# Expert weights loaded per tile as the stationary operand, hidden activations made transposed, and shared-expert units regrouped

## The reference, cut to what matters

```python
x = x + tanh(g_xattn) * attention(layernorm(x), ctx)      # 8192 tokens x 128
flat = layernorm(x)
scores = softmax(flat @ router_w.T + router_bias)         # 32 experts
topk_scores, topk_idx = top_k(scores, 4)                  # normalised to sum 1
h = silu(flat @ gate_w[e].T) * (flat @ up_w[e].T)         # width 128, per expert e
expert_out = h @ down_w[e].T
out = sum over the token's four experts of topk_score * expert_out
out = out + silu(flat @ sgate_w.T) * (flat @ sup_w.T) @ sdown_w.T   # shared, width 512
x = x + tanh(g_ffn) * out
```

## Time and profile before

| | us |
|---|---|
| runs | 1081.31, 1076.92, 1077.49; median 1077.49 |
| the profiled execution | 1076.78, its span 1074.9 |
| attention | 0 to 565 |
| early stage | 565 to 592 |
| expert loop, to the last scatter | 592 to 997 |
| late stage | 997 to 1075 |

### The profile page before, as it was taken

The page is one execution under the profiler, slowest core; times in us unless marked ns, Lnnn a source line. Parts: engine busy times, 40 slices in busy tenths (PEclk is TensorE's granted clock), DMA queues, the critical chain, the costliest instruction groups (busy, mean ns, idle before and its releaser), DMA issues.

```text
span 1074.9 us, 26031 instructions
## 1 busy us (share of the span) xinstructions
PE 954.3 (89%) x6592; PEld 728.6 (68%) x6593; DVE 733.7 (68%) x2496; ACT 613.1 (57%) x2213; POOL 669.9 (62%) x935
## 2 busy tenths in 40 slices
PE   4988888988888888889769999999999999999987
PEld 2777777777777777777655666666667666776544
DVE  3788888888888988888755344444444444454696
ACT  3667766767677777767532455555555555555211
POOL 1267777777777777777662477677777677777100
PEclk9999999999999999999879899999999999999999
DMA  5511111111111111111315433333333333331794
GB/s 154 200 37 33 36 37 37 33 33 39 36 36 33 39 38 33 39 38 62 110 33 98 99 96 95 95 91 90 94 93 96 93 92 93 93 94 32 273 363 146
DMA packets 91623, 90.43 MB, mean 84 GB/s; under 512 B 21277, under 2 KB 73098, under 8 KB 91204
## 3 DMA queue, kind: packets, MB, share of 16 engines
q1 hardware_dynamic: 71876, 55.07, 18.4%
q0 software_dynamic: 17408, 33.87, 9.6%
q10 hardware_dynamic: 2304, 1.07, 0.6%
HBM read 49.72 MB, written 42.31 MB: 86 GB/s over the span
## 4 chain that ended last, share of the span: by engine, by line
PE 43%; DVE 17%; issue 16%; DMA 12%; POOL 9%; ACT 1%; POOLq 1%; SPq 0%; DVEq 0%; ACTq 0%
DMA x_rows<-payload,slot 11%; PE ps L1071 11%; POOL x_rows L432 9%; PE ps L1082 9%; DVE payload L751 3%; PE ps L1108 3%; PE ps L1066 3%; PE ps L1076 3%; PE ps L1092 3%; PE ps L1098 3%; PE ps L1035 2%; DVE kvbd L677 2%; PE ps L942 2%; DVE w_gu L881 1%; PE ps L1044 1%
## 5 line engine op out<-in xcount | busy, mean ns | idle before, releaser
L443 POOL DMA_INDIRECT y_rows<-y_sb,xin x288 | 283.0, 983 | 141.8 <-issue 80.5
L432 POOL DMA_INDIRECT x_rows<-payload,slot x256 | 251.2, 981 | 132.7 <-DVE slot L762 70.4
L836 DVE TENSOR_TENSOR h<-sg,ps 128x128 f32<-128x128 f32 x288 | 82.6, 287 | 181.6 <-ACT sg L575 181.6
L1071 PE MATMUL ps<-w_gu,xT 128*128 x576 | 175.9, 388 | 8.2 <-issue 8.2
L1082 PEld LDWEIGHTS ps<-w_dn,hT 128*128 128x128 f32 x576 | 94.4, 190 | 105.8 <-ACT hT L580 73.0
L942 PE MATMUL ps<-vt,pT 128*128 128x108 f32 x1024 | 145.6, 287 | 0.0
L580 ACT COPY hT<-ps 128x128 f32<-128x128 f32 x288 | 76.4, 265 | 109.7 <-PE ps L1076 107.4
L942 PEld LDWEIGHTS ps<-vt,pT 128*128 128x128 f32 x1024 | 130.7, 200 | 11.3 <-issue 10.9
L1082 PE MATMUL ps<-w_dn,hT 128*128 x576 | 129.9, 308 | 8.1 <-DVE y_sb L842 6.2
L575 ACT ACTIVATE sg<-ps 128x128 f32<-128x128 f32 x288 | 80.5, 280 | 72.7 <-PE ps L1071 48.8
L842 DVE TENSOR_SCALAR y_sb<-ps,xin 128x128 f32<-128x128 f32 x288 | 99.7, 346 | 24.2 <-PE ps L1082 22.5
(11 more groups left out here) (136 smaller groups left out, 1978.4 us busy)
## 6 DMA issues: line engine op xcount, KB each, us to landing
xin<-x_rows SPq DMA_DIRECT2D x288, 65.0 KB, 1.9
w_gu<-y_rows SPq DMA_DIRECT2D x16, 1024.0 KB, 8.6
y_rows<-y_sb,xin POOLq DMA_INDIRECT x288, 2.3
w_gu<-in_gu SPq DMA_DIRECT2D x2, 2048.0 KB, 10.3
x_rows<-payload,slot POOLq DMA_INDIRECT x256, 2.4
out<-x_all SPq DMA_DIRECT2D x16, 256.0 KB, 5.8
w_dn<-in_dn SPq DMA_DIRECT2D x1, 2048.0 KB, 8.8
ctx_sb<-in_ctxT SPq DMA_DIRECT2D x64, 29.2 KB
```

The lines of the kernel that those rows point to most:

```text
L432: nc.gpsimd.indirect_dma_start(x_rows, bass.IndirectOffsetOnAxis(ap=slot[:, v, k:k + 1], axis=0), payload[:, v, k, :], None).then_inc(sent ...
L443: nc.gpsimd.indirect_dma_start(y_rows, bass.IndirectOffsetOnAxis(ap=xin[:, u, D:D + 1].bitcast(U32), axis=0), y_sb[:, u, :], None, bounds_ ...
L836: nc.vector.tensor_tensor(h[:, u % 2, :], sg[:, u % 2, :], ps_gu[u % 2][:, H:2 * H], ALU.mult).then_inc(h_d[u % PER], 1)
L1071: after(nc.tensor.matmul(ps_gu[u % 2][:, 0:2 * H], xT[:, u % 2, :], w_gu[:, bass.ds(e * (2 * H), 2 * H)], start=True, stop=True), xT_d, n, ...
```

## The change

**Weights per tile.** `w_gu` and its two loads are gone. `w_t` (in a new tensor `moe`, on which the result slots lie too) has 18 slots of 256 columns. For each tile SyncE issues a load of that expert's 128 KB, then the load of `xin`; both raise the same semaphore, so its counts go by 32. A row reads 18 first rows and 21 expert numbers. The first row is split: tiles 0 to 3 first, then 4 to 17.

**Transposed hidden.** `gate_up` is two products now, with the weights stationary and `xT` moving, so that the hidden activations come out transposed. `turn_h` on TensorE and the copy `h_turned` on ScalarE are gone. Three banks and buffers (`DEEP` = 3) take turns instead of two. `down` and `result` come for the tile three before the current gate/up, and ahead of it in the order.

**Shared units.** `EARLY` is 1, `MID` 11. Four units stand in a row, at tiles 1, 5, 9 and 13, one whole chunk per row, in rows 1 to 6 and 8 to 12. Rows 0, 7, 13, 14 and 15 have none. Four chunks are left for the late stage.

**Paddings and scatters.** ScalarE issues four paddings per early unit instead of two; SyncE issues 12 before the table is stored and 4 after (before 8 and 8). GpSimd waits for each tile's result instead of for every second.

```diff
-EARLY = 2
-MID = 8
+EARLY = 1
+MID = 11
-UNIT_AT = (6, 14)
+DEEP = 3
+UNIT_AT = (1, 5, 9, 13)
...
         def bodies(body, fori):
-            body(0, 0, 0, first=True)
-            body(1, 0, 1)
-            with fori(1, MID - 1) as c:
-                body(2 * c, c, 0)
-                body(2 * c + 1, c, 1)
-            body(TG - 2, MID - 1, 0)
-            body(TG - 1, MID - 1, 1, last=True)
+            body(0, first=True)
+            with fori(1, 7) as j:
+                body(j, chunk=EARLY - 1)
+            body(7)
+            with fori(8, 13) as j:
+                body(j, chunk=EARLY - 2)
+            with fori(13, TG - 1) as j:
+                body(j)
+            body(TG - 1, last=True)
...
-                     2: lambda: sp.dma_start(w_gu[:, 0:half], gu[:, 0:half]).then_inc(s_moe, 16),
-                     3: lambda: sp.dma_start(w_gu[:, half:], gu[:, half:]).then_inc(s_moe, 16),
...
-            def load_tiles(j):
-                firsts = numbers(sp, tab_sb, j * TW, U3, XROWS - 128)
-                for u in range(U3):
+            def load_tiles(j, begin=0, end=U3):
+                firsts = numbers(sp, tab_sb, j * TW + begin, end - begin, XROWS - 128)
+                es = numbers(sp, tab_sb, j * TW + EAT + begin, end - begin + 3, E - 1)
+                for u in range(begin, end):
                     need(sp, y_sent[u], 16 * j)
-                    sp.dma_start(xin[:, u, :], x_rows[bass.ds(firsts[u], 128), :]).then_inc(xin_in[u], 16)
-            load_tiles(0)
+                    sp.dma_start(w_t[:, u, :], gu[:, bass.ds(es[u - begin + 3] * (2 * H), 2 * H)]).then_inc(xin_in[u], 16)
+                    sp.dma_start(xin[:, u, :], x_rows[bass.ds(firsts[u - begin], 128), :]).then_inc(xin_in[u], 16)
+            load_tiles(0, 0, 4)
+            load_tiles(0, 4, U3)
...
             def scatter(n, u):
-                if u % 2 == 0:
-                    need_first(pool, y_d[(u + 1) % PER], n[(u + 1) // PER + 2])
+                need_first(pool, y_d[u % PER], n[u // PER + 2])
...
-            def gate_up(n, u, e):
-                after(nc.tensor.matmul(ps_gu[u % 2][:, 0:2 * H], xT[:, u % 2, :], w_gu[:, bass.ds(e * (2 * H), 2 * H)],
-                                       start=True, stop=True), xT_d, n, u).then_inc(gu_p[u % PER], 1)
+            def gate_up(n, u):
+                after(nc.tensor.matmul(ps_gu[u % DEEP][:, 0:H], w_t[:, u % U3, 0:H], xT[:, u % 2, :],
+                                       start=True, stop=True), xT_d, n, u)
+                nc.tensor.matmul(ps_gu[u % DEEP][:, H:2 * H], w_t[:, u % U3, H:2 * H], xT[:, u % 2, :],
+                                 start=True, stop=True).then_inc(gu_p[u % PER], 1)
...
             def body(j, first=False, last=False, chunk=None):
                 n = counts(dve, j, U3 // PER)
                 for u in range(U3):
+                    if not (first and u < 3):
+                        result(n, u - 3)
                     hidden(n, u)
-                    if not (first and u < 2):
-                        result(n, u - 2)
-                    if u - 2 in UNIT_AT:
-                        mixed_hidden(c, 2 * half + UNIT_AT.index(u - 2))
-                if half:
-                    mixed_take(c)
+                    if chunk is not None and u - 1 in UNIT_AT:
+                        mixed_hidden(j + chunk, UNIT_AT.index(u - 1))
+                if chunk is not None:
+                    mixed_take(j + chunk)
```

More of the change, by code:

```diff
@@ L332, in _ @@
             sp.dma_start(tab_dram, tab[0:TG, :]).then_inc(t_store, 16)
-            with sp.Fori(2, PADS_SP // 4) as e:
-                paddings(e)
+            paddings(PADS_SP // 4 - 1)
             sp.wait_ge(t_store, 16)
@@ L559, in _ @@
             for n in range(4 * EARLY):
-                if n % 2 == 0:
-                    firsts = numbers(act, basei, PADS_SP + 2 * n, 4, XROWS - 128)
-                for first in firsts[2 * (n % 2):2 * (n % 2) + 2]:
+                for first in numbers(act, basei, PADS_SP + 4 * n, 4, XROWS - 128):
                     act.dma_start(x_rows[bass.ds(first, 128), :], pad[:, :]).then_inc(t_padded2, 16)
@@ L574, in silu, with mixed_silu @@
                 tile_done(act, gu_p, n, u)
[L575 to L583, removed]
+                nc.scalar.activation(sg[:, u % DEEP, :], ps_gu[u % DEEP][:, 0:H], ACT.Silu).then_inc(sg_d[u % PER], 1)
+            def mixed_silu(c, k):
+                unit = 4 * c + k
                 need(act, sg_p, 2 * unit + 1)
@@ L586, in mixed_silu, with body @@
                 nc.scalar.activation(ssg[:, k % 2, :], ps_g[:, :], ACT.Silu).then_inc(ssg_d, 1)
-            def body(j, c, half, first=False, last=False):
+            def body(j, first=False, last=False, chunk=None):
                 n = counts(act, j, U3 // PER + 1)
@@ L591, in body @@
                     silu(n, u)
-                    if not (first and u == 0):
-                        h_turned(n, u - 1)
                     if not (last and u >= U3 - 2):
                         evac(n, u + 2)
-                    if u in UNIT_AT:
-                        mixed_silu(c, 2 * half + UNIT_AT.index(u))
+                    if chunk is not None and u in UNIT_AT:
+                        mixed_silu(j + chunk, UNIT_AT.index(u))
             for u in range(2):
@@ L857, in mixed_take, with body @@
                                                op0=ALU.mult, op1=ALU.add).then_inc(take_d, 4)
-            def body(j, c, half, first=False, last=False):
+            def body(j, first=False, last=False, chunk=None):
                 n = counts(dve, j, U3 // PER)
                 for u in range(U3):
+                    if not (first and u < 3):
+                        result(n, u - 3)
                     hidden(n, u)
-                    if not (first and u < 2):
-                        result(n, u - 2)
-                    if u - 2 in UNIT_AT:
-                        mixed_hidden(c, 2 * half + UNIT_AT.index(u - 2))
-                if half:
-                    mixed_take(c)
+                    if chunk is not None and u - 1 in UNIT_AT:
+                        mixed_hidden(j + chunk, UNIT_AT.index(u - 1))
+                if chunk is not None:
+                    mixed_take(j + chunk)
             bodies(body, dve.Fori)
-            for u in range(2):
-                result(counts(dve, TG), u - 2)
+            for u in range(3):
+                result(counts(dve, TG), u - 3)
             def combine(c):
@@ L1079, in down, with units @@
             def down(n, u, e):
                 tile_done(pe, y_d, n, u - 1)
-                after(nc.tensor.matmul(ps_dn[:, 0:D], hT[:, u % 2, :], w_dn[:, bass.ds(e * D, D)], start=True,
+                after(nc.tensor.matmul(ps_dn[:, 0:D], hT[:, u % DEEP, :], w_dn[:, bass.ds(e * D, D)], start=True,
                                        stop=True), hT_d, n, u).then_inc(dn_p[u % PER], 1)
-            def units(j, k):
-                unit = 4 * (EARLY + j) + k
+            def units(c, k):
+                unit = 4 * c + k
```

104 lines of the change are left out of this document (48 added, 56 removed).

## The result

The changed kernel takes 1096.1 us (median of four runs, 1090.72 to 1098.5); the kernel before took 1079.4 beside it. The ratio is 1.0143, with a 95% interval of 1.0088 to 1.0197: slower by 1.4%, where 1082 us, 0.4%, was forecast. The measured median lies outside the forecast's own 1073 to 1092 and inside the range for 8 in 10, 1056 to 1098, near its upper end.

What follows compares the result with a forecast made beforehand. Expert loop bound by TensorE in chunk rows, GpSimd in others: from 617.5, rows to 943.2, last scatter 1015.4, tail 63.5, end 1078.9; with 1.9 around it and the median's footing, 1082 us. Range 1073 to 1092; 8 in 10, 1056 to 1098.

Steps and rivals of the forecast that it cites:

- rival B: In the expert loop SyncE's loads become the bound, from 0.67 us per load: rows take 27.9, total 1098; chance 0.18.
- A unit's four tiles: In the expert loop, four tiles with a shared unit, delayed by VectorE's wait, take 6.2 to 6.3 us.
- the delayed down: In a unit's group, TensorE's down waits for a result behind VectorE's product: 4.44 us, where it was due at 4.03.
- Rival A: In the expert loop VectorE's wait does not delay the down: groups take 5.7 us, rows 25.6, total 1057; chance 0.27.
- Rival C: In the late stage TensorE waits some 8 us for the first combine, returning at 0.50 clock: total 1087; chance 0.05.
- The tail: From the last scatter to the end, with fewer late units and an earlier first combine: 63.5 us instead of 78.0.
- The start: Before the steady loop: first load near 588.5, about 1.8 us gained; row 1's first tile taken at 617.5.
- from 617.5: In the loop's sum, row 1's first tile starts then; eleven chunk rows and row 7 follow, ending at 943.2.
- Chunk rows: The eleven expert-loop rows with four shared units each: 27.6 to 28.1 us, taken as 27.9.
- plain row 7: The expert-loop row without shared units, between the chunk rows: TensorE takes 18.8 us.
- the ring: Plain tiles' chain from gate/up to the next but one: 1.96 us for two; a row above 20 disproves it.
- From row 13's first gate product to its first scatter: Near the loop's end, three tiles, down, result and issue put the first scatter about 4 us later.

## Why the prediction was right, and what it mis-sized

**The range was held in part by luck.** The forecast alone, with its own terms, ended at 1092; 1096.1 is beyond it. The range for 8 in 10 reached to 1098 because it went to half of rival B, and B did not happen. That the change is slower had 0.46; the forecast value of 0.4% was itself within the 0.5% that the prediction counted as no change.

**The mechanism held.** A unit's four tiles were put at 6.2 to 6.3 and measure 6.32; the tile with the gate 1.63 and 1.64; the delayed down at 4.44 from the group's start and 689.98 - 685.43 = 4.55. L841 starts 0.13 after the up product's end where 0.05 was counted; the difference is about the 0.1 that was priced for register instructions. Rival A needed groups under 5.9 and falls by the rows; the runs with the product later (-18 us) and with two banks (-26 us, against the 25 that A was priced at) show what it would have been; the second also shortens plain tiles, as shown below. Rival B needed SyncE as long as TensorE's row: a row of 36 loads takes 22.4 to 22.7 where SyncE isn't held up, as forecast with 22.3, and 0.52 per load, and with the same loads the rows fall to 23.2 in two of the runs. The Trainium skill's rule for large transfers (DMA: Bandwidth & Descriptors, section Measured (HBM→SBUF, 128 partitions, SWDGE, issued from GpSimd)) does not decide here: the run without the bytes is as slow. Rival C was half there: TensorE did wait for the first combine, but for 3.27 us instead of some 8 (1037.61 above); until 1034.3 it had its late units to do. In this window the clock stayed at its 2.4 GHz level, 1.00 (columns as above):

```profile
1034.00:1042.00 8.00, 4.43 (x22) 2.76 (x22) 7.55 (x10) 0.72 (x2) 0.00 (x0) 1.00 1.03 379
```

The tail was put at 63.5 and is 62.5.

**What was mis-sized is the loop, by 11 us of the profiled span** (1078.9 forecast, 1088.9 measured, with 1.0 back from the tail):

- The start, 3.3. The first load was put at 588.5 and came at 589.88, though the attention's last scatter was 0.9 earlier; in all ten kernels here it comes 17.6 to 19.0 after that scatter, where 588.5 meant 16.4. This cost the sum nothing, since it took the later of its two cases: the second row's loads were due at 611.7 + 3.2 = 614.9 and began at 614.30. What the step "from 617.5" left out comes behind them. In TensorE's order the transposes of the row's first two tiles stand ahead of its first gate product. The second waits for its load until 618.55, and from there to the gate product are 2.25 more: 620.80.
- Chunk rows, 4.6. They were put at 27.9 and take 28.3 on the mean. Four groups are 25.3, so 2.9 to 3.1 are left in most rows for two more tiles, the row's start and the take, where 2.85 were counted. With 6.3 per group the forecast's own terms add up to 28.05, and 27.9 was taken.
- The plain row 7, 1.7, which takes TensorE 20.5 instead of 18.8 (18 x 0.98 + 1.03 is 18.7). A plain row above 20 was to prove the ring wrong, and it came. The ring itself is short by 0.03 per tile, as the rows below show, which makes 0.6. The rest lies at the row's edges: the second reading of numbers, 0.92 in TensorE's queue, holds up one tile by 0.6 and was not counted, and the row's first tile and the change to the next row add 1.65 where 1.0 was counted.
- From row 13's first gate product to its first scatter, 1.3: 5.3 instead of 4.

Here are two plain tiles of row 7, from a gate product (L1061) to the next but one:

```profile
793.31 0.39 PE L1061 MATMUL ps<-xT,moe 128*128 128x128 f32 x2
...
794.00 0.48 PE L1069 MATMUL ps<-w_dn,hT 128*128 x2
...
794.52 0.35 DVE L833 TENSOR_SCALAR y_sb<-ps,xin 128x128 f32<-128x128 f32 x1
...
795.01 0.48 PE L1069 MATMUL ps<-w_dn,hT 128*128 x2
...
795.33 0.39 PE L1061 MATMUL ps<-xT,moe 128*128 128x128 f32 x2
```

The forecast's ring takes 2.02 for two tiles instead of 1.96: VectorE's result starts 1.21 after the gate product, not 1.15; the 0.49 and 0.32 behind it are as forecast. A second ring closes in the same 1.01 per tile, which the forecast did not name: a down (794.00), its result 0.52 later, the next down 0.49 after that. Which of the two sets the tile can't be told from these rows; both pass through the one bank. With two banks the plain tiles of the same row are (789.13 - 784.11)/6 = 0.84 apart, so the one bank prices plain tiles as well as units:

```profile
784.11 0.39 PE L1062 MATMUL ps<-xT,moe 128*128 128x128 f32 x2
...
789.13 0.39 PE L1062 MATMUL ps<-xT,moe 128*128 128x128 f32 x2
```

**The rest, some 5 us, lies outside the profiled execution.** The median of the four executions is 5.4 above the profiled one, and the forecast was made on the footing of a profile 0.7 below the median. In the ten profiled executions of all kernels here the attention's last scatter starts between 569.9 and 578.3, though the code of that stage is the same but for the two weight loads; from there to the end the change and the three runs that gave nothing all take 517 to 518 us, the kernel before 502.8. The three longer executions of the change have a lower granted clock over the whole span, 0.956 to 0.960 instead of 0.965. They were not profiled, so that they lost their time in the attention is likely, and not shown.

## What to carry to other kernels

An instruction that waits in an in-order queue charges everyone behind it: before a product is moved nearer to its producer, look at what stands next on that engine and who waits for that, and through which buffer. Background work was free here up to the pace of the slowest engine in each row (23.2 us) and dear beyond it, so it is better spread evenly to that pace than gathered in a few rows. A buffer that has one slot is worth a look even where no wait is large: here a second bank took 0.17 off a plain tile and 0.49 off the four tiles of a unit. A load that lands a row ahead may move many bytes for nothing.

## What the runs showed of the hardware that was not expected

In the attention most batches take 8.1 us, but between six and twelve take 8.8 to 11.0. There are two kinds.

The 29th and the 57th are long in all ten profiled executions, 10.0 to 10.1 and 10.2 to 11.0 us. In the change GpSimd stands 2.2 us instead of 0.30 before the second scatter of both, for a reason that the profile doesn't show. The clock is not the cause: it is at its 2.4 GHz level through the 29th batch of the change (first its late scatter, then the window of the batch, columns as above).

```profile
280.45 0.97 POOL L435 DMA_INDIRECT x_rows<-payload,slot  x1 [2.17 <-issue]
```

```profile
277.00:287.00 10.00, 7.34 (x67) 6.10 (x66) 7.67 (x31) 6.25 (x21) 6.06 (x10) 1.00 0.09 30
```

The others lie at other places in each execution. In the one from 345 to 354 of the change, of 9.2 us, all scatters are on time, but for 3 us TensorE runs at its 1.2 GHz level, busy throughout:

```profile
347.00:350.00 3.00, 3.00 (x16) 3.00 (x16) 2.47 (x9) 1.53 (x6) 2.38 (x4) 0.50 0.15 49
```

TensorE had stood 1.53 for VectorE just before. It stands about 1.5 in nearly every fourth batch and less in the others. Between 100 and 510 us of the change the clock fell behind three of these waits (346.50, 380.29, 413.97) and once behind one of 1.14 (288.55); it stayed at 1.00 behind others of 1.5 (213.96, 313.89, 447.48). What decides between them stays open. What the long batches take over 8.1 us adds up to 8.2 and 8.4 us in the two profiled executions whose attention ends first (571.2 and 569.9, the change and the run without the bytes) and to 15.0 in the one where it ends last (578.3, the run with one early chunk): more than several terms of the forecast.
